# The first cross-attention without barriers at its two ends: the first batch's keys turned under the last query pair, the output product behind the context

## The reference

```python
q_hk = (hidden_q @ Wq.T).reshape(Bv, Sv, H, K)
q_big = einsum('bshk,hkq->bshq', q_hk, w_kc_q)
q_big = rope(q_big); kv_r = rope(kv_c)
q_r = einsum('bshq,hqr->bhsr', q_big, W_qr)
k_r = einsum('bld,hdr->bhlr', kv_r, W_kr)
attn = softmax(einsum('bhsr,bhlr->bhsl', q_r, k_r), axis=-1)
ctx_c = einsum('bhsl,bld->bhsd', attn, kv_r)
ctx_lat = einsum('bhsd,hkd->bhsk', ctx_c, w_kc_kv)
return ctx_lat.transpose(0, 2, 1, 3).reshape(Bv, Sv, H * K) @ Wo.T
...
x = x + _L0_xattn_ref(_layernorm(x), ctx_512, ...)
x = x + _L0_ffn_ref(_layernorm(x), ...)
```

## Time and profile before

| | us |
|---|---|
| median of 3 runs | 1382.12 |
| lowest, highest | 1380.94, 1385.76 |
| the profiled execution | 1389.93 |
| its span in the trace | 1388.1 |
| PE busy | 1267.8 (91%) |
| DVE, ACT, POOL busy | 812.3, 616.7, 820.8 |

### The profile page before, as it was taken

How to read it: one execution, slowest core, us unless ns; L and a number is a source line. 1 busy time by engine, 2 the same in 40 slices (tenths; PEclk the granted TensorE clock), 3 DMA queues, 4 the chain that set the end, 5 groups by cost and what they waited for, 6 DMA issues and landing times.

```text
span 1388.1 us, 20144 instructions
## 1 busy us (share of the span) xinstructions
PE 1267.8 (91%) x7051; PEld 824.3 (59%) x7051; DVE 812.3 (59%) x1444; ACT 616.7 (44%) x1644; POOL 820.8 (59%) x747
## 2 busy tenths in 40 slices
PE   7999998999999999999988576998999998989792
PEld 4865545666666666666657563444777884547582
DVE  5756666666766667666733626776666214764443
ACT  4731113544444444445440323888766025872151
POOL 1266005999999999999990534888544003660444
PEclk9999997999999999999998786999999999998897
DMA  8501110000000000000008320000000105200263
GB/s 259 134 9 38 31 38 19 9 9 12 9 9 9 8 13 9 9 9 9 12 1 276 86 80 27 0 1 1 1 1 1 27 0 154 62 2 31 69 141 118
DMA packets 67532, 60.12 MB, mean 43 GB/s; under 512 B 19440, under 2 KB 64392, under 8 KB 66920
## 3 DMA queue, kind: packets, MB, share of 16 engines
q1 hardware_dynamic: 64408, 50.56, 13.2%
q0 software_dynamic: 3024, 8.26, 2.5%
HBM read 40.58 MB, written 9.83 MB: 36 GB/s over the span
## 4 chain that ended last, share of the span: by engine, by line
PE 76%; POOL 7%; DVE 6%; ACT 6%; issue 3%; DMA 1%; another core or an unknown queue 0%; POOLq 0%; DVEq 0%; SPq 0%; ACTq 0%
PE PS L481 71%; PE PS L489 4%; ACT s_sc L1300 2%; POOL PWS L1934 2%; POOL a_m L1994 2%; POOL a_m L1988 2%; DVE s_mx L1719 1%; ACT a_m L1257 1%; DVE HN L1402 1%; POOL slot_rows L1974 1%; DVE pm L1511 1%; PE PS L638 1%; PE PS L675 0%; DVE stats L1392 0%
## 5 line engine op out<-in xcount | busy, mean ns | idle before, releaser
L1934 POOL TENSOR_TENSOR PWS<-PWS 128x1024 f32<-128x1024 f32 x160 | 379.2, 2370 | 46.1 <-ACT PWS L1196 26.8
L1511 DVE TENSOR_REDUCE pm<-PS 128x2 f32<-128x1024 f32 x192 | 226.1, 1221 | 106.4 <-PE PS L481 106.3
L1196 ACT ACTIVATE PWS<-PS 128x512 f32<-128x512 f32 (+1 forms) x416 | 212.7, 600 | 79.0 <-PE PS L481 73.9
L481 PE MATMUL PS<-PWS,KVR 128*64 128x256 f32 (+1 forms) x1664 | 185.2, 379 | 0.0
L481 PE MATMUL PS<-QALL,KH 128*128 128x512 f32 (+1 forms) x416 | 181.3, 436 | 0.1
L481 PE MATMUL PS<-QM,KL 68*128 68x512 f32 (+1 forms) x416 | 166.1, 399 | 0.0
L2009 POOL TENSOR_SCALAR s_sc<-s_sc,s_ri 128x128 f32<-128x128 f32 (+1 forms) x256 | 103.9, 425 | 93.4 <-DVE s_ri L1726 93.4
L481 PEld LDWEIGHTS PS<-PWS,KVR 128*64 128x64 f32 (+1 forms) x1664 | 121.4, 137 | 58.2 <-issue 0.2
L481 PEld LDWEIGHTS PS<-QALL,KH 128*128 128x128 f32 (+1 forms) x416 | 77.1, 185 | 76.7 <-ACT PWS L1196 58.9
L1300 ACT ACTIVATE s_sc<-PS,s_nb 128x128 f32<-128x128 f32 (+1 forms) x256 | 104.6, 434 | 4.5 <-DVE s_nb L1722 4.5
L1202 ACT ACTIVATE CTX<-PS 128x256 f32<-128x256 f32 x32 | 12.3, 385 | 194.5 <-PE PS L481 194.5
(11 more groups left out here) (307 smaller groups left out, 2377.2 us busy)
## 6 DMA issues: line engine op xcount, KB each, us to landing
QALL<-qlo SPq DMA_DIRECT2D x32, 128.0 KB, 2.4
QM<-QALL SPq DMA_DIRECT2D x64, 64.0 KB, 2.0
f_w<-in_L_ffn_w_dram SPq DMA_DIRECT2D x2, 2048.0 KB
tile_results<-e_y SPq DMA_DIRECT2D x31, 128.0 KB
a_nat<-in_L_attn_w_qkv_dram SPq DMA_DIRECT2D x1, 3072.0 KB, 22.0
x_wq<-in_L_xattn_Wq_dram SPq DMA_DIRECT2D x1, 2048.0 KB, 10.4
x_wo<-in_L_xattn_Wo_dram SPq DMA_DIRECT2D x2, 1024.0 KB, 7.4
a_wo<-in_L_attn_w_o_dram SPq DMA_DIRECT2D x1, 2048.0 KB, 21.1
```

Of the source, the lines that this page charges most:

```text
L481: return nc.tensor.matmul(o, a, b, start=start, stop=stop, **kw)
L1196: nc.scalar.activation(PW[c][0:rows, j * HALF:(j + 1) * HALF], st_bank("block", LT * u + lt)[0:rows, :], ACT.Exp).then_inc(p_ready, 1)
L1511: V.tensor_reduce(pm[u % 2][:, :, i // 3, i % 3], src, AX, ALU.max).then_inc(nat_read, 1)
L1934: G.tensor_tensor(ACC[:, :], PW[0][:, :] if i == 0 else ACC[:, :], PW[i + 1][:, :], ALU.add).then_inc(acc_step, 1)
```

## The change

`PsumBanks` can be told to go on at a given bank, with nobody to wait for (`start_at`). The barriers' later numbers go down by one.

At the front, barrier 2 is taken out. The bank order of the query phase is shifted so that its last group has bank 7. The four key banks of batch 0 are claimed and filled between z(15) and q(14); ACT copies them ahead of query group 14, DVE takes the differences ahead of `lows(14)`. Plain score 0 waits for the high parts of group 14 and the emptied third key bank, plain score 1 for group 14's bank; the first tail waits for the last group's bank, the pads and the moved query rows. POOL sets the pads of the first pair of tiles ahead of the end of the phase and those of the second pair behind the last query group. SP waits for the last group's bank.

At the end, barrier 3 is split: every engine drains and counts when it is through, and only SP waits for all four, for its loads. PE goes on with output products 0 and 1, then makes the last unit's weight sums, then products 2 to 5. Each product waits for `norm_done` of the batches that it reads. DVE does the last unit's reciprocal and scaling between its additions for tiles 1 and 2. `normalised` has a semaphore of its own for the reciprocal.

```diff
@@ PsumBanks
+    def start_at(self, bank):
+        self.base, self.first = len(self.order), bank
...
-        self.jobs[key] = (len(self.order), by, self.count[by])
+        self.jobs[key] = (len(self.order), by, self.count[by], (self.first + len(self.order) - self.base) % 8,
+                          self.order[-8] if len(self.order) - self.base >= 8 else None)
@@ PE
+            def first_keys():
+
+                pe.wait_ge(dup_ready, 2)
+                for q in range(4):
+                    ps = begin(("k", q), "dve")
+                    for i, lt in enumerate(range(4 * q, min(4 * q + 4, LT))):
+                        w = P if lt < LT - 1 else LREST
+                        last = nc.tensor.transpose(ps[:, i * P:i * P + w], DUP[0:w, lt, :], ident[0:w, 0:w])
+                    last.then_inc(filled, 1)
+
             wait_ht(1)
+            banks.start_at(len(banks.order) % 8 + 4)
             z_jobs(0)
             for n in range(2 * PAIRS):
                 if n + 1 < 2 * PAIRS:
                     z_jobs(n + 1)
+                if n == 2 * PAIRS - 2:
+                    first_keys()
                 q_job(n)
-            ended(pe, 2)
...
                 if n == 0:
-                    pe.wait_ge(rows_set, 1)
-                    for s in range(2):
-                        pe.wait_ge(q_moved[s], 32 * PAIRS)
+                    pe.wait_ge(q_high, 2 * (2 * PAIRS - 1))
+                    pe.wait_ge(*banks.emptied(("k", 2)))
+                if n == 1:
+                    pe.wait_ge(*banks.emptied(("q", PAIRS - 1, 0)))
...
+                if u == 0:
+                    pe.wait_ge(*banks.emptied(("q", PAIRS - 1, 1)))
+                    pe.wait_ge(rows_set, 1)
+                    for s in range(2):
+                        pe.wait_ge(q_moved[s], 32 * PAIRS)
                 ps = st_begin("tail", u)
...
-            for q in range(4):
-                keys(0, q)
...
-            weight_sums(UNITS - 1)
-            ended(pe, 3)
+            pe.drain().then_inc(phase_ended, 1)
+            banks.start_at(3)
+
             def attended(t):
 
+                if t == 0:
+                    pe.wait_ge(nat_read, PLAINS * UNITS)
+                if t == 4:
+                    pe.wait_ge(ctx_read, UNITS)
+                pe.wait_ge(norm_done, PAIRS * (t // 2 + 1) if t < 5 else UNITS - 1 if t == 5 else UNITS)
                 out_product(("xo", t), [(CTX[:, p, t * P:(t + 1) * P], U[:, p, :]) for p in range(PAIRS)])
...
-            for t in range(6):
+            for t in range(2):
+                attended(t)
+            weight_sums(UNITS - 1)
+            for t in range(2, 6):
                 attended(t)
             turn_half(0)
@@ ACT
             for n in range(2 * PAIRS):
                 p, half = n // 2, n % 2
+                if n == 2 * PAIRS - 2:
+                    for q in range(4):
+                        act.wait_ge(*banks.filled(("k", q)))
+                        w = min(HALF, L - q * HALF)
+                        nc.scalar.activation(KH[0][:, q * HALF:q * HALF + w], banks.bank(("k", q))[:, 0:w], ACT.Copy).then_inc(kh_ready, 1)
...
-            ended(act, 3)
+            act.drain().then_inc(phase_ended, 1)
             deviations(2, 0)
@@ DVE
                     rotate(n + 1)
+                if n == 2 * PAIRS - 2:
+                    for q in range(4):
+                        ps = banks.take(("k", q), "dve")
+                        dve.wait_ge(kh_ready, q + 1)
...
+                        V.tensor_tensor(KL[0][0:D, cols], ps[0:D, 0:w], KH[0][0:D, cols].bitcast(F32),
+                                        ALU.subtract).then_inc(emptied["dve"], 1)
                 lows(n)
-            ended(dve, 2)
...
-                link(V.reciprocal(sums, sums))
+                V.reciprocal(sums, sums).then_inc(inv_ready, 1)
+                dve.wait_ge(inv_ready, u + 1)
...
-            normalised(UNITS - 1)
-            ended(dve, 3)
+            dve.drain().then_inc(phase_ended, 1)
 
             def attended(t):
+                if t == 2:
+                    normalised(UNITS - 1)
@@ POOL
             doubled(0)
-            ended(pool, 2)
...
+            pool.wait_ge(w1_split, PAIRS)
+
+            def pads_set(i):
+                for k in (KH[i], KL[i]):
+                    link(G.memset(k[:, L:L + 1].bitcast(F32), 0.0))
+                G.memset(KL[i][64:68, :].bitcast(F32), 1.0).then_inc(rows_set, 1)
+
+            pads_set(0)
+            pool.wait_ge(rows_set, 1)
+            pool.wait_ge(*banks.emptied(("q", PAIRS - 1, 1)))
+            pads_set(1)
+            pool.wait_ge(rows_set, 2)
...
-            ended(pool, 3)
+            pool.drain().then_inc(phase_ended, 1)
@@ SP
-            sp.wait_ge(phase_ended, 4 * 2)
+            sp.wait_ge(*banks.emptied(("q", PAIRS - 1, 1)))
...
-            sp.wait_ge(phase_ended, 4 * 3)
+            sp.wait_ge(phase_ended, 4 * 2)
```

More of the change, by code:

```diff
@@ L53, in __init__ @@
         self.taken = {e: 0 for e in emptied}
+        self.base, self.first = 0, 0
+    def start_at(self, bank):
+        self.base, self.first = len(self.order), bank
     def claim(self, key, by):
@@ L62, in bank @@
     def bank(self, key):
-        n = self.jobs[key][0] % 8
+        n = self.jobs[key][3]
         return self.psum[:, n * 512:(n + 1) * 512]
     def earlier(self, key):
-        n = self.jobs[key][0]
-        return self.order[n - 8] if n >= 8 else None
+        return self.jobs[key][4]
     def filled(self, key):
@@ L73, in emptied @@
     def emptied(self, key):
-        _, by, n = self.jobs[key]
+        by, n = self.jobs[key][1:3]
         return self.emptied_sem[by], n
@@ L419, in plains_after @@
                     for a, z in ((4, 6), (6, 8), (8, 10))]
-        ST_ITEMS = [("keys", 0, q) for q in range(4)] + [("tail", 0), ("maxima", 0)]
+        ST_ITEMS = [("tail", 0), ("maxima", 0)]
         for u in range(UNITS):
@@ L443, in st_freed @@
             kind, *at_ = ST_ITEMS[n]
-            return {"keys": lambda: (kl_ready, 4 * at_[0] + at_[1] + 1), "maxima": lambda: (qm_ready, at_[0] + 1),
+            return {"keys": lambda: (kl_ready, 4 * (at_[0] - 1) + at_[1] + 1), "maxima": lambda: (qm_ready, at_[0] + 1),
                     "block": lambda: (p_ready, at_[0] + 1), "tail": lambda: (tail_read, at_[0] + 1),
@@ L830, in _ @@
             turn_x(3)
-            ended(pe, 4)
+            ended(pe, 3)
             def qkv(n):
@@ L852, in _ @@
                 qk_turn(n)
-            ended(pe, 5)
+            ended(pe, 4)
             def softmax_units(tag, units, turnable, score, use):
@@ L925, in _ @@
             turn_x(4)
-            ended(pe, 6)
+            ended(pe, 5)
             for ct in range(KC):
@@ L1065, in _ @@
                 shared_down(t)
-            ended(pe, 7)
+            ended(pe, 6)
         @block.scalar
@@ L1243, in _ @@
             ht_out(3)
-            ended(act, 4)
+            ended(act, 3)
             def qk_out(n):
@@ L1276, in _ @@
                     qk_out(n - 4)
-            ended(act, 5)
+            ended(act, 4)
             def softmax_units(tag, units, base_n, scale):
@@ L1317, in _ @@
             turned_norm(4)
-            ended(act, 6)
+            ended(act, 5)
             for ct in range(KC):
@@ L1365, in _ @@
             nc.scalar.activation(f_e[:, :, :], f_e[:, :, :], ACT.Exp).then_inc(e_exp, 1)
-            ended(act, 7)
+            ended(act, 6)
         @block.vector
@@ L1672, in _ @@
             ht_out(3)
-            ended(dve, 4)
+            ended(dve, 3)
             def table(a):
@@ L1709, in _ @@
             V.tensor_copy(s_identb[:, :], ident[:, :]).then_inc(mask_set, 1)
-            ended(dve, 5)
+            ended(dve, 4)
             def softmax_units(tag, units, base_n, scale, after):
@@ L1740, in _ @@
             turned_norm(4, added("ao"))
-            ended(dve, 6)
+            ended(dve, 5)
             def y_after(n, unit):
@@ L1853, in _ @@
                 V.scalar_tensor_tensor(X[:, t, :], e_yg[:, t, 1, :], e_w[:, 1, t:t + 1], X[:, t, :], ALU.mult, ALU.add).then_inc(x_final, 1)
-            ended(dve, 7)
+            ended(dve, 6)
         @block.gpsimd
@@ L1982, in _ @@
                                      bounds_check=last_slot, oob_is_err=False).then_inc(res_back[t], 16)
-            ended(pool, 4)
+            ended(pool, 3)
             def rotated(n):
@@ L2000, in _ @@
                     biased(n - 2)
-            ended(pool, 5)
+            ended(pool, 4)
             G.memset(y_v[:, :, :, :, :], 0.0).then_inc(v_cleared, 1)
@@ L2024, in _ @@
             masked_keys(0)
-            ended(pool, 6)
+            ended(pool, 5)
             masked_keys(1)
```

31 lines of the change are left out of this document (15 added, 16 removed).

## The result

The changed kernel took 1381.28 us (median; 1370.64 to 1383.22), the kernel before, run beside it, 1385.79 (1380.51 to 1391.14). The ratio is 0.9948, with an interval of 0.9931 to 0.9964: **7.2 us less** (5.0 to 9.6), where 10.2 were forecast. 3.7 of the 9.4 us are the level of the kernel before: the three runs shown had put it at 1382.12, these runs put it at 1385.79. By the ratio, taken run beside run, the gain fell 3.0 us short (10.2 against 7.2). The last 2.7 us are the difference between the two ways to state the gain, since the medians differ by only 4.5 us; I go by the ratio. The times of the changed kernel fall into two groups, nine from 1370.6 to 1377.3 and eleven from 1381.1 to 1383.2; why is a question for the end.

A forecast was written before the change was run, and what follows sets the result against it. TensorE was taken to bound the kernel, with 76% of the span. Front 2.8 plus end 7.4 gave 10.2 us: profiled 1389.93 becomes 1379.7, and 7.8 lower for the median, 1371.9, range 1368.0 to 1377.5.

The forecast's parts named there:

- the level of the kernel before: Whole kernel: the unchanged kernel's median was taken as 1382.12 us, 7.8 below its profiled execution.
- the half-clock term of the front: First unit's maxima and turned scores: PE's half clock costs some 2 us, assumed unchanged.
- The end: Behind the attention: output products follow the context directly, a_wo's load then binds, second logits copy 7.4 us earlier (5.1 to 9.1).
- Rival B: Behind the load wait: PE's clock stays half through the logits, giving 1374.2 us; chance 0.18.
- C: Loads behind the attention: the slot rows' zero fill makes a_wo land later, giving 1375.5 us; chance 0.08.
- D: Behind the attention: the loads don't bind, a_wo being earlier than thought, giving 1368.2 us; chance 0.06.
- The front: Ahead of the attention: key transposes cost 1.5 us, first maxima start 2.8 us earlier; range -1.1 to +4.8.
- The covers of ACT, DVE, POOL and SP: Front: these engines' moved copies, differences, memsets and waits fit into idle time or delay nobody.
- the forecast's own price: First unit: each us of dense PE work at half clock loses 0.5 us.
- the bound "2.5 lost if it lasted 9 us": Front: lower end for the half-clock stretch, 2.5 us lost if it lasted 9 us.
- Rival E: Front yields nothing: moved transposes run at half clock, half-clock stretch grows some 3 us, giving 1374.7 us; chance 0.05.

The follow-up runs named there:

- the pair: One profiled execution each of the kernel before and the changed kernel, compared: 1389.93 and 1381.46 us.
- end only: Kernel before with only its last barrier split, barrier 2 and the key transposes behind it kept: 1378.07 us, ratio 0.9919.
- after late: Changed kernel in which PE waits for the first unit's tenth maximum ahead of the first turned score: ratio 0.9933.
- busy maxima: Changed kernel plus 15 unread products on PE between the first unit's plain scores and ahead of its turned maxima: 1372.89 us, ratio 0.9885.
- two small fillers: Changed kernel plus two short unread products, ahead of plain scores 8 and 9 of the first unit: ratio 0.9928.
- loads by need: Changed kernel with the loads behind the attention issued in order of need, with separate semaphores: 1373.88 us, ratio 0.9897.
- front only: Changed kernel with barrier 3 put back and the last weight sums ahead of it: 1383.73 us, ratio 0.9984; second sample 1386.93 us or near, see its one execution.
- before late: Kernel before in which PE waits for the first unit's tenth maximum ahead of the first turned score: ratio 1.0015.
- after late again: Second sample of the changed kernel with PE waiting for the tenth maximum ahead of the first turned score: one execution, 1386.93 us.
- before late again: Second sample of the kernel before with PE waiting for the tenth maximum ahead of the first turned score: one execution, 1396.44 us.

## Why the prediction was wrong, and where it was right

The step that failed is the half-clock term of the front, "the change leaves this stretch sparse and I keep its cost", some 2 us. The changed front paid 5.2 us for it on average and up to 7.3, so that the front's 2.8 us became about nothing. The second miss is the level of the kernel before, 3.7 us. The order of events at both ends came as forecast.

**The end: right, step by step.** The stretch became 7.16 us shorter in the pair and 7.4 in end only against a forecast of 7.4. Products straight behind the context (725.88), the last weight sums between the second and the third (732.95), the loads free when POOL is through (731.71; POOL's last addition, begun at 730.35, takes 1.26 us and ends 0.1 us before), a_wo landing 20.8 us after its issue, PE idle for 5.21 us where 5.6 were forecast (4.9 to 6.2 in the other traces with that wait), 16 transposes at half clock in 3.66 (3.5 forecast), logits at full clock in 2.13 (1.97). DVE's last reciprocal and scaling slipped between its additions for tiles 1 and 2, as said.

**Rival B, half clock behind the load wait, did not come.** The 16 transposes at 762.71 began at half clock, and the logits at 768.08 took 2.13 (their weight loads 2.07), against 3.49 for the weight loads of the same 16 in before. The windows of after 764 to 770 us:

```profile
764.00:766.00 2.00, 2.00 (x12) 2.00 (x11) 0.00 (x0) 1.49 (x3) 0.00 (x0) 0.50 1.04 356
766.00:768.00 2.00, 1.25 (x10) 1.00 (x8) 0.00 (x0) 1.74 (x4) 0.00 (x0) 0.94 0.64 226
768.00:770.00 2.00, 1.92 (x16) 1.95 (x17) 0.00 (x0) 0.00 (x0) 0.00 (x0) 0.91 0.03 12
```

PE had done nothing but transposes since its idle time when the clock rose to 0.94. The Trainium skill, "TensorE: Matmul & The Clock Gate", Part 4 (PE-mode transpose), says that full clock does not engage for transposes; this trace and the earlier trace rows (209 to 214 us) both show the opposite, and the measurement decides. B lost every time, not only here: in all eight traces in which PE stood for a_wo (after three times, after late twice, end only, busy maxima, two small fillers) these 16 logits took 1.92 to 2.25 us. Loads by need had them at half clock (3.55), though its pause of 2.32 us was shorter than this one of 5.21, and so had before and front only, each twice. The difference in the traces is what PE did in between: 24 transposes behind the long wait, 8 behind the short one. No run varies the two apart.

**C and D.** The zero fill did not delay a_wo (20.8 us, 21.1 before). The loads did bind, as the run with loads by need showed; without them the stretch is 2.3 us shorter, not 3.7 as D had it, because DVE's normalising beside POOL's clearing was the next limit. The forecast had not looked at what stood behind a_wo, and its own rows had it: PE idle for 2.38 us for `HN` ahead of the second turned half.

**The front: the earlier start right, the half-clock term mis-sized.** The transposes cost 1.37 us (1.5 forecast). In the pair the first maxima came 2.66 us after the last query copy started, not 6.96: 4.3 less, and with the transposes 2.8 to 2.9 gained up to there. The covers of ACT, DVE, POOL and SP held. What failed is the step "Half clock: ... the change leaves this stretch sparse and I keep its cost". The cost, "some 2 us", was not kept. Full clock had come back 3.8 us behind the first turned scores, and now it came back after 9.8, 16.9, 9.9, 3.8, 13.4 and 13.5 us. By the forecast's own price, half a us for each us of unbroken work at half clock, the 6 us more of the profiled pair lose 3, and the pair's table shows 2.65 (29.38 - 4.3 + 2.65 = 27.73). Over the six traces the stretch is 28.25 against 29.42 for three of before (before twice, end only): 1.2 us less, with 1.4 to 1.5 us of transposes ahead of it. **The front yields about nothing** by these nine traces, and with that 10.2 becomes 7.4, which agrees with the ratio (7.2, with 5.0 to 9.6). The cost that came, some 3 us more than the 2 kept, lies beyond even the bound "2.5 lost if it lasted 9 us". Rival E had named this result and given it a chance of 1 in 20, for a cause of which half was right: the longer half clock, not dearer transposes.

**The level of before** was the other miss: a median of three runs, 1382.12, in a kernel whose runs spread over 11 us. A range that is set around three runs must be wider by what three runs don't know. With the level right, the forecast would have been 1375.6, and the gain by the ratio, taken from 1382.12, would have lain inside the range (1374.9).

**What stays open.** That the front's loss is the time at half clock is shown: products under the maxima take all of it away (23.02), and the stretches follow the length of the half clock from run to run. What sets that length is not. That it hangs on the moment at which the unbroken work starts accounts for before late, after late and after late again; against it stand two small fillers and before late again. That the change prolongs the half clock in itself, by leaving PE idle ahead of and between the scores, isn't ruled out either. The length was some 4 us in all three traces of before's undelayed front and in one of six of the changed one; so few don't rule out chance. Nor was it tried why the third stretch, which most of these kernels leave as it is, takes 602.6 to 616.6 us; the half clock at 1164 to 1184 us in after, 1.00 there in before, shows one place where it comes and goes. The clock is the likely cause of the two groups of times as well: the mean granted clock was 0.951 or 0.952 in each of the eleven slower executions of after and 0.954 to 0.961 in each of the nine faster ones. Which stages make the difference isn't known, since only one of the twenty has a trace.

## What to carry to other kernels

Taking a barrier away moves the wait to what the barrier had hidden: look for the loads that were issued behind it, order them by need, and then ask what stands next (here a normalising beside memsets). Removing idle time ahead of a sparse stretch brings little while TensorE falls to half clock in it; keeping it busy through the gap worked in the changed kernel (0.9885) and did not behind the barrier, with fewer products (1.0005), so look at the granted clock before and after adding them. And cost a half-clock stretch from several traces, not by the length that one happens to show.

## What the runs showed of the hardware

- TensorE stayed at half clock through up to 16.9 us of unbroken work in this stage, and through 20 us of it at 1164 to 1184 us in after. The same kernel (front only) got its clock back after 3.8 us in one execution and after 13.4 in another. The longest stretch with PE busy at half clock that the trace of before had shown was 9 us.
- Full clock came back behind PE work that was transposes alone: 13 of them at 209.17 us in before, 16 and some of the 8 behind them at 762.71 in after.
- Normalising four tiles took DVE 1.38 us with POOL idle, 3.97 us beside POOL's clearing, and 2.34 with half of the clearing moved. The Trainium skill, "SBUF — State Buffer", Who interferes with whom, speaks of a port pair that DVE and POOL share and lock for a whole instruction. The traces agree in so far as a single one of the four took up to 2.03 us in after, where it takes 0.41 undisturbed; that the ports are the reason, no run here shows.
